# Causal attention in a six-layer kernel: the mask moves from TensorE products to GpSimd selects, and narrow score tiles share a PSUM bank

## The reference

```python
qkv = jnp.einsum('bsd,hde->bhse', x, Wqkv) + bqkv[None, :, None, :]
q, k, v = jnp.split(qkv, 3, axis=-1)
score = jnp.einsum('bhsd,bhtd->bhst', q, k)
causal = jnp.tril(jnp.ones((s, s), dtype=bool))
score = jnp.where(causal[None, None], score, -jnp.inf)
attn = jax.nn.softmax(score / jnp.sqrt(jnp.asarray(HEAD_DIM, x.dtype)), axis=-1)
y = jnp.einsum('bhst,bhtd->bhsd', attn, v)
y = jnp.transpose(y, (0, 2, 1, 3)).reshape(b, s, d)
out = y @ Wout + bout
```

## Time and profile before

| | |
|---|---|
| time, median of 3 runs | 1552.42 us (1550.23 to 1552.64) |
| time of the profiled execution | 1552.19 us |
| its span | 1550.4 us |
| busy over the span: PE, DVE, ACT, POOL | 94%, 64%, 49%, 29% |
| the layer's interleaved part | about 690 to 972 us of the span |
| exponentials L2232 | 384, 164.7 us busy |
| maxima L2277 | 304, 181.4 us busy |

### The profile page before, as it was taken

The page is one execution under the profiler, slowest core; times in us unless marked ns, Lnnn a source line. Parts: engine busy times, 40 slices in busy tenths (PEclk is TensorE's granted clock), DMA queues, the critical chain, the costliest instruction groups (busy, mean ns, idle before and its releaser), DMA issues. The chain is left out here.

```text
span 1550.4 us, 19613 instructions
## 1 busy us (share of the span) xinstructions
PE 1458.8 (94%) x7170; PEld 859.1 (55%) x7170; DVE 988.1 (64%) x1506; ACT 762.3 (49%) x1317; POOL 454.1 (29%) x348
## 2 busy tenths in 40 slices
PE   6999999989999899879999999899889999999998
PEld 3757765423232365444545443323568888888886
DVE  5774244778877634448887773677577574664753
ACT  5566345533434642725666665434655544445442
POOL 0046430142221410370000000201236656655562
PEclk9999999999999999989999999999999999999999
DMA  7000000000000000191553300000413222223201
GB/s 292 1 0 0 1 4 1 0 1 1 1 1 0 1 0 1 48 142 16 132 68 50 43 2 1 4 1 0 137 41 106 72 82 100 78 70 107 73 10 55
DMA packets 39047, 67.59 MB, mean 44 GB/s; under 512 B 3944, under 2 KB 19368, under 8 KB 38568
## 3 DMA queue, kind: packets, MB, share of 16 engines
q1 hardware_dynamic: 38952, 66.33, 16.1%
HBM read 57.80 MB, written 8.39 MB: 43 GB/s over the span
## 5 line engine op out<-in xcount | busy, mean ns | idle before, releaser
L2232 ACT ACTIVATE arena<-psum 128x512 f32<-128x512 f32 (+3 forms) x384 | 164.7, 498 | 118.8 <-PE psum L2082 85.1
L2277 DVE TENSOR_REDUCE b_mx<-psum 128x1 f32<-128x512 f32 (+3 forms) x304 | 181.4, 653 | 57.0 <-PE psum L2058 47.4
L3021 POOL TENSOR_TENSOR m_w_rest<-m_w,m_w_high 128x512 fp32r<-128x512 f32 (+1 forms) x88 | 111.6, 1270 | 154.7 <-ACT m_w_high L3220 154.7
L3471 DVE TENSOR_TENSOR m_hidden<-m_gelu,psum 128x512 f32<-128x512 f32 (+1 forms) x88 | 60.4, 686 | 147.7 <-ACT m_gelu L3312 124.5
L3114 PE MATMUL psum<-m_x_high,m_w_high 128*128 128x512 f32 (+1 forms) x352 | 137.9, 392 | 3.2 <-issue 3.2
L3027 POOL TENSOR_TENSOR m_h_rest<-m_hidden,m_h_high 128x512 fp32r<-128x512 f32 (+1 forms) x88 | 122.1, 1388 | 59.0 <-ACT m_h_high L3234 59.0
L3114 PE MATMUL psum<-m_x_rest,m_w_high 128*128 128x512 f32 (+1 forms) x352 | 137.7, 391 | 0.0
L3114 PE MATMUL psum<-m_x_high,m_w_rest 128*128 128x512 f32 (+1 forms) x352 | 137.6, 391 | 0.0
L3312 ACT ACTIVATE m_gelu<-psum 128x512 f32<-128x512 f32 (+1 forms) x88 | 52.4, 596 | 119.7 <-PE psum L3114 119.7
L1359 ACT ACTIVATE x_probs<-psum 128x1024 f32<-128x1024 f32 x56 | 57.3, 1023 | 90.4 <-PE psum L1097 90.4
L1517 DVE TENSOR_REDUCE x_mx<-psum 128x2 f32<-128x1024 f32 x64 | 76.6, 1218 | 35.0 <-PE psum L1071 34.8
(11 more groups left out here) (594 smaller groups left out, 3252.7 us busy)
## 6 DMA issues: line engine op xcount, KB each, us to landing
m_w<-w SPq DMA_DIRECT2D x32, 512.0 KB, 4.5
m_wo<-wo SPq DMA_DIRECT2D x16, 512.0 KB, 4.0
weights_sb<-weights SPq DMA_DIRECT2D x2, 2820.0 KB, 12.3
m_w<-w SPq DMA_DIRECT2D x16, 344.0 KB, 4.6
b_q_stack<-b_q_dram SPq DMA_DIRECT2D x36, 128.0 KB, 6.0
b_k_stack<-b_k_dram SPq DMA_DIRECT2D x36, 128.0 KB, 5.9
weights_sb<-weights SPq DMA_DIRECT2D x1, 3328.0 KB, 14.3
b_q_dram<-b_q_parts SPq DMA_DIRECT2D x6, 512.0 KB, 3.4
```

Of the source, the lines that this page charges most:

```text
L2232: act.activation(probs[slot % RING][:, 0:n], score(slot)[:, 0:n], ACT.Exp, scale=SCALE).then_inc(s["expd"].sem)
L2277: dve.tensor_reduce(mx[:, part, qi, heads[0]:heads[0] + nh], tile(("piece", p))[:, 0:nh * keys].rearrange("p (h n) -> p h n", n=keys), AX, ...
L3021: pool.tensor_tensor(w_rest[:, n % W_RING, :, :, 0:H_N(n % HT)], raw_of(n), w_high[:, n % W_RING, :, :, 0:H_N(n % HT)].bitcast(F32), ALU.s ...
L3471: dve.tensor_tensor(hidden[rows, n % 2, :], gelu[rows, n % 2, :], c.bank(2 + n % 2)[rows, :], ALU.mult)\
```

## The change

The product with `past` (L2082), and `past` itself, are gone. In its place GpSimd sets the exponentials of the future to zero: for each of the 64 diagonal groups one `affine_select` over the first 128 columns of its four tiles (128 x 4 x 128, f32, in place), after the group's last exponential and, by a new semaphore `masked`, ahead of its `values`.

Slots of 256 columns now share a bank two by two, and those of 128 four by four: `score_tiles` lists groups with the heads of one tile. One exponential takes the whole tile. A tile is issued at the slot of its first head; the slots of its other heads keep only what else stood there. So 304 exponentials take the place of 384. The three squares of GpSimd now stand among its selects.

```diff
--- before.py
+++ after.py
@@ -1782,6 +1782,11 @@
 
     groups = [(hs, ki) for hs in range(HALVES) for ki in range(4 * (hs % 2) + 4)]
     width = lambda ki, half: (half + 1) * CH - max(ki * P, half * CH)
+    diagonal_upto = lambda g: sum(ki >= 4 * (hs % 2) for hs, ki in groups[:g + 1])
+    together = lambda g: CH // width(groups[g][1], groups[g][0] % 2)
+    score_tiles = [(g, range(x, x + together(g))) for g in range(len(groups)) for x in range(0, QUAD, together(g))]
+    tiles_upto = lambda g: sum(of <= g for of, _ in score_tiles)
+    tile_at = {(g, heads[0]): i for i, (g, heads) in enumerate(score_tiles)}
     pairs_upto = lambda hs: 6 * (hs // 2) + (2 if hs % 2 == 0 else 6)
     first_group = lambda hs: 2 * pairs_upto(hs - 1) if hs else 0
 
@@ -1873,6 +1877,8 @@
         qs = [q_stack[:, 0], q_stack[:, 1], spare[:, 0]]
         ks = [k_stack[:, 0], k_stack[:, 1], spare[:, 1]]
         probs = [c.arena[:, i * CH:(i + 1) * CH] for i in range(RING)]
+        quad_of = lambda g: c.arena[:, QUAD * g % RING * CH:(QUAD * g % RING + QUAD) * CH].rearrange("p (h n) -> p h n", h=QUAD)
+        assert RING % QUAD == 0
         o, ot = c.slot(4), c.slot(5)
         o_t = o.rearrange("p a n -> p (a n)").rearrange("p (t n) -> p t n", t=TT)
         heads_out = c.ln[:].rearrange("p a n -> p (a n)")[:, 0:CH]
...
@@ -1962,13 +1968,10 @@
             def _(pool):
                 pool.memset(v_aug, 1.0).then_inc(s["ones"].sem)
                 c.clear_stale(pool)
-                pool.memset(future[:], 0.0)
-                pool.memset(past[:], 0.0).then_inc(s["masks"].sem)
+                pool.memset(future[:], 0.0).then_inc(s["masks"].sem)
                 pool.wait_ge(*s["masks"](1))
                 pool.affine_select(out=future[:], in_=future[:], compare_op=ALU.is_ge, fill=NEG, base=0,
-                                   pattern=[[-1, P]], channel_multiplier=1)
-                pool.affine_select(out=past[:], in_=past[:], compare_op=ALU.is_ge, fill=NEG, base=0,
-                                   pattern=[[1, P]], channel_multiplier=-1).then_inc(s["masks"].sem)
+                                   pattern=[[-1, P]], channel_multiplier=1).then_inc(s["masks"].sem)
                 pool.wait_ge(*s["masks"](2))
                 pool.memset(k_stack[ROWS:ROWS + SHIFT, :, :, :], 1.0).then_inc(s["k_ones"].sem)
                 for done in stored:
@@ -1987,11 +1990,28 @@
                 pool.wait_ge(*pr["v_proj"](8))
                 pool.memset(ks[2][ROWS:ROWS + SHIFT], 1.0).then_inc(s["k_ones"].sem)
                 pool.wait_ge(*s["k_ones"](2))
-                for ch in range(3):
+
+                def mask_future(g):
+
+                    pool.wait_ge(*s["expd"](tiles_upto(g)))
+                    to = quad_of(g)[:, :, 0:P]
+                    pool.affine_select(out=to, in_=to, compare_op=ALU.is_ge, fill=0.0, base=0,
+                                       pattern=[[0, QUAD], [1, P]], channel_multiplier=-1).then_inc(s["masked"].sem)
+
+                def next_square(ch):
                     pool.wait_ge(*s["read"](nth["mean", ch] + 1))
                     if ch == 2:
                         pool.wait_ge(*s["made"](nth["var", 0] + 1))
                     pool.tensor_tensor(next_squares(ch), chunk(xn_all, ch), chunk(xn_all, ch), ALU.mult).then_inc(yn["sq"].sem)
+
+                for g, (hs, ki) in enumerate(groups):
+                    if hs == HALVES - 2 and ki == 3:
+                        next_square(0)
+                    if ki >= 4 * (hs % 2):
+                        mask_future(g)
+                    if hs == HALVES - 2 and ki == 3:
+                        next_square(1)
+                next_square(2)
 
             @block.tensor
             def _(pe):
@@ -2065,27 +2085,28 @@
                         mm = pe.transpose(rows[:, t * P:(t + 1) * P], shift[:, hs % 2, t, :], ident16)
                     mm.then_inc(s["made"].sem)
 
-                def scores(slot):
-                    (hs, ki), h = groups[slot // QUAD], slot % QUAD
+                def scores(i):
+                    g, heads = score_tiles[i]
+                    hs, ki = groups[g]
                     a, half = hs // 2 % 3, hs % 2
-                    if ki == 0 and h == 0:
+                    if ki == 0 and heads[0] == 0:
                         pe.wait_ge(*shifted[hs % 2](SHIFT * 16 * (hs // 2 + 1)))
                         if hs == 4:
                             pe.wait_ge(*s["k_ones"](2))
-                    if slot >= SCORES:
-                        pe.wait_ge(*s["expd"](slot - SCORES + 1))
+                    if i >= SCORES:
+                        pe.wait_ge(*s["expd"](i - SCORES + 1))
                     q0, n = max(ki * P, half * CH), width(ki, half)
-                    diagonal = ki >= 4 * half
-                    mm = pe.matmul(score(slot)[:, 0:n], ks[a][0:ROWS + SHIFT, h, ki * P:(ki + 1) * P],
-                                   qs[a][0:ROWS + SHIFT, h, q0:q0 + n], start=True, stop=not diagonal)
-                    if diagonal:
-                        mm = pe.matmul(score(slot)[:, 0:P], ident16, past[:], start=False, stop=True)
+                    for x, h in enumerate(heads):
+                        mm = pe.matmul(score(i)[:, x * n:(x + 1) * n], ks[a][0:ROWS + SHIFT, h, ki * P:(ki + 1) * P],
+                                       qs[a][0:ROWS + SHIFT, h, q0:q0 + n], start=True, stop=True)
                     mm.then_inc(s["scored"].sem)
 
                 def values(pair):
                     hs, first_ki = groups[2 * pair]
                     b, quad, half = part_of(hs)
-                    pe.wait_ge(*s["expd"](QUAD * (2 * pair + 2)))
+                    pe.wait_ge(*s["expd"](tiles_upto(2 * pair + 1)))
+                    if first_ki >= 4 * half:
+                        pe.wait_ge(*s["masked"](diagonal_upto(2 * pair + 1)))
                     if first_ki == 0 and hs >= 1:
                         pe.wait_ge(*s["out_copied"](hs))
                     for i in range(2):
@@ -2148,7 +2169,8 @@
                 pe.wait_ge(*pr["v_copied"](8))
                 for slot in range(QUAD * len(groups)):
                     (hs, ki), x = groups[slot // QUAD], slot % QUAD
-                    scores(slot)
+                    if (slot // QUAD, x) in tile_at:
+                        scores(tile_at[slot // QUAD, x])
                     more_pieces(upto[slot], upto[slot + 1])
                     if x == QUAD - 1 and ki % 2 == 1 and slot // QUAD >= 3:
                         values(slot // QUAD // 2 - 1)
...
@@ -2223,13 +2245,16 @@
                 for t2 in range(4):
                     copy_value(1, t2)
 
-                def exps(slot):
-                    (hs, ki), h = groups[slot // QUAD], slot % QUAD
+                def exps(i):
+                    g, heads = score_tiles[i]
+                    hs, ki = groups[g]
                     n = width(ki, hs % 2)
-                    act.wait_ge(*s["scored"](slot + 1))
-                    if slot >= RING:
-                        act.wait_ge(*s["av"]((slot - RING) // QUAD // 2 + 1))
-                    act.activation(probs[slot % RING][:, 0:n], score(slot)[:, 0:n], ACT.Exp, scale=SCALE).then_inc(s["expd"].sem)
+                    act.wait_ge(*s["scored"](i + 1))
+                    if g >= RING // QUAD:
+                        act.wait_ge(*s["av"]((g - RING // QUAD) // 2 + 1))
+                    act.activation(quad_of(g)[:, heads[0]:heads[-1] + 1, 0:n],
+                                   score(i)[:, 0:len(heads) * n].rearrange("p (h n) -> p h n", n=n), ACT.Exp, scale=SCALE)\
+                       .then_inc(s["expd"].sem)
 
                 def copy_out(hs):
                     act.wait_ge(*s["av"](pairs_upto(hs)))
@@ -2239,7 +2264,8 @@
 
                 for slot in range(QUAD * len(groups)):
                     (hs, ki), x = groups[slot // QUAD], slot % QUAD
-                    exps(slot)
+                    if (slot // QUAD, x) in tile_at:
+                        exps(tile_at[slot // QUAD, x])
                     if hs >= 1 and ki == 2 and x == 1:
                         copy_out(hs - 1)
                 copy_out(HALVES - 1)
```

More of the change, by code:

```diff
@@ L1847, in causal_attention_layer @@
                                        loaded0=0, loaded1=0, loaded2=0, shifted0=0, shifted1=0, made=0, read=0,
-                                       max_step=0, parts=0, scored=0, expd=0, av=0, out_copied=0, inv=0))
+                                       max_step=0, parts=0, scored=0, expd=0, masked=0, av=0, out_copied=0, inv=0))
         set_round(0, s, pr)
@@ L1855, in causal_attention_layer @@
         future = sb("b_future", [P, P], BF16)
-        past = sb("b_past", [P, P], BF16)
         q_parts = sb("b_q_parts", [P, 3, FT, S], BF16)
@@ L1890, in causal_attention_layer @@
         norm_bank = lambda ch: c.bank(4 + ch)
-        score = lambda slot: c.bank(slot % SCORES)
+        score = lambda i: c.bank(i % SCORES)
         out_tile = c.bank(SCORES)
@@ L1915, in loads @@
```

(4 more changed lines are left out.)

## The result

The changed kernel takes 1534.15 us (1533.49 to 1545.4, 4 runs) against 1551.33 (4 runs), a ratio of 0.9903 with a 95% interval of 0.9881 to 0.9925. Forecast were 1536 us and 16.3 us less; 17.2 us less were measured. In a later comparison it was 1536.72 against 1553.86, 0.9892 (0.9877 to 0.9907).

What follows compares the result with a forecast made beforehand. PE's stream was taken to bound six of eight steps. Six steady steps gave 13.7 us, step 0 1.15 and step 7 1.46, together 16.3 us less: 1536 us, range 1532 to 1544.

Steps and rivals of the forecast that it cites:

- PE sets the pace: Steady steps: PE, busy 31.13 of 31.44 us, sets their time; each step saves 2.28 us.
- Wide products at 58 ns: Groups 512 and 384 wide: 16 products with past gone from PE, 0.93 us a step, less 0.1 for ACT.
- End of the even half: Narrow groups there: PE turns 0.43 us sooner and two masked scores go, 0.23 more; 0.66 us saved a step.
- End of the odd half: Narrow groups there: 2.41 us shrink to 1.62, ACT taking no part; 0.79 us saved a step.
- GpSimd's selects at nothing: Diagonal groups: a select takes 0.69 us, 0.7 to 1.4 with bounds, covered everywhere including the layer's end; cost 0.
- DVE at nothing: Steps: DVE's work stays 25.17 us and costs nothing, with 0.5 us a step as the bound.
- The rival by which a select shuts DVE out: Splitting of the shift held up by selects, up to 16.6 us, so no change, 1552; chance 0.06.
- Step 0: First step: nothing gained in the even half, where DVE sets the pace; 1.15 us in the odd one.
- End of the layer: Step 7's odd half: 0.35 us from products ahead of the projections, 0.45 from three heads behind the norm's product.
- The slower rival: Values of wide pairs wait for dearer selects: 16 us per microsecond beyond about 2.8, 1560 at 4.3; chance 0.07.

Runs made afterwards that it cites:

- e5: Changed kernel with the 256 products that mask the pieces left out too, maxima taken over the whole diagonal block: 1526.62 us, 0.9849.
- e1: Changed kernel without the shared tiles: every head has its own tile and exponential, GpSimd's selects stay in place of the products: 1544.25 us, 0.9959.
- e2: Changed kernel with the shared tiles alone: the products with past stay, no selects: 1544.51 us, 0.9957.
- e3: Changed kernel without the selects and the wait for them, exponentials of the future left in, so the mask is wrong: 1535.12 us, 0.9896.
- x3: Changed kernel with each of the 64 selects done three times, one after the other: 1543.0 us, 0.9949.
- x5: Changed kernel with each select done five times: 1604.39 us, 1.0339.
- e6: Changed kernel with the turning of the half before and its division moved from slot 1 to slot 3 of group 3: 1535.04 us, 0.9899.
- e7: Changed kernel with both maxima over the whole diagonal block and the turning moved to slot 3 of group 3: 1526.41 us, 0.9838.
- x3b: Changed kernel with each select done three times, but once in the last half: 1538.92 us, 0.9906.

## Why the prediction was right

The direction, the mechanism and the size held. Step by step:

- *PE sets the pace.* Shown. The steady steps lost 2.15 us each (forecast 2.28), with PE as full as before; e5 shows that this ends some 1 us further down.
- *Wide products at 58 ns.* Forecast 0.93 less 0.1 for ACT; measured 0.47 + 0.32 = 0.79. The odd half falls short of 0.46 by 0.14, where ACT and PE were forecast as level. ACT runs its eight exponentials there without a gap, 3.73 us from 793.40, which fits; no run makes ACT faster to show it.
- *End of the even half.* Forecast 0.66, measured 0.54. The term that was off is the turning: 1.66 us from the first score in place of 1.55. ACT's copy starts where it was forecast, 0.93 us behind the first score (0.92 before), and ends at 779.05; but PE turns only at 779.19, 0.14 later, where the sum had 0.03 for the way from ACT to PE.
- *End of the odd half.* Forecast 0.79, measured 0.81. e1 and e2 show that it needs both parts: 0.22 and 0.33 alone.
- *GpSimd's selects at nothing.* Shown by e3, and the cover by x3 for the steady steps. Forecast 0.69 us each, measured 0.64. At the end of the layer the cover is too thin for three selects, as x3 shows; a single one fits in it.
- *DVE at nothing.* It held in the steps. The rival by which a select shuts DVE out is real as a mechanism, below, but in the changed kernel the selects hardly meet the splitting: the one instruction that they hold up is the first of an odd half (L2314), 216 ns in place of 176, and PE's wait for the shift at the passage to the eighth step is 1.74 us with the selects and 1.70 without (e3). The prediction has it that no row before the change shows the mechanism; one does, that of L2291 in the last section.
- *Step 0.* From the first piece to ACT's first copy 45.9 us before and after (674.7 to 720.6; 683.6 to 729.5), though the clock was 0.89 there before and 0.85 after: this half gained nothing, as forecast. That DVE's own work sets its pace is only part of it. DVE stands still for 3.66 us of it before (3.90 after) beside GpSimd, and e5, with the same maxima, took 41.7.
- *Missed: 1.5 us at the passage to the eighth step.* From ACT's copy in the seventh step's odd half to that in the eighth's the sum had 1.81 (0.36 + 0.79 of the one half, 0.66 of the other), and it gave 3.31. Some 1.6 of that is the clock, for which the sum had no term. The steps' 0.13 each too much, 0.7 to 0.8 in six, hid half of it. So it is luck that the total, 17.0 us in the layer against 16.3, is nearer to the forecast than its terms; with the clock alike in both kernels it would have been about 15.4, still in the range.
- *End of the layer.* Forecast 0.35 + 0.45 = 0.80, measured 0.72 (from ACT's copy in the last half to the next layer, 31.16 us before and 30.44 after).
- *The slower rival's price.* It had 16 us for each microsecond over the cover. x5 shows it too low for a wait of this length: 2.6 us of waiting cost 4.3, as the clock falls behind the wait.

## What to carry to other kernels

Where PE's starts follow one another without holes, a small product costs the distance to the next start (58 ns for 128 columns here, though its record lasts 220), and moving it to an engine that stands still is worth that, if the new engine's result is wanted only much later; count the cover from the last input to the first use, and count it at the end of a stage apart, where nothing stands in between. Two edits that take away different limits of one place, here the product and the wait for a bank, give more together than alone. A wait put on TensorE is to be priced with what its clock may do behind it, and a gain of a microsecond or two is to be looked up in the clock of both profiles before the change gets it. Idle time on an engine isn't free room for another when the two can shut each other out: look what long instructions stand beside a short one that others wait for.

## What was not expected of the hardware

A wait of PE of 1.2 to 2.6 us can be followed by some microseconds at half the clock: 7 us at 0.50 in x3, 0.64 over 3.5 us in x5, 0.56 over 3.5 us in the kernel before. It doesn't have to be, and the length of the wait doesn't tell. At one and the same place, PE's wait for the shift at the passage to the eighth step, the profiles have:

| | PE waits, us | clock behind the wait |
|---|---|---|
| before, both profiles | 1.51, 1.50 | falls to 0.50 |
| e1, e2 | 1.50, 1.50 | 1.00 |
| changed, both profiles | 1.74, 1.74 | 1.00 |
| e3 | 1.70 | 1.00 |
| e6 | 1.73 | falls to 0.50 |
| e5 | 1.90 | 1.00 |
| e7 | 1.90 | falls to 0.50 |
| x3b | 2.16 | 1.00 |
| x3 | 2.16 | falls to 0.50 |

The fall lasts 3 to 4 us each time. What decides is open.

A short DVE instruction does stand still beside one of GpSimd. The same line (the splitting, `b_shift` from `b_mx` and `b_shift`, two SBUF inputs) in the changed kernel and in x3, where selects run beside it more of the time:

```profile
L2319 DVE SCALAR_TENSOR_TENSOR b_shift<-b_mx,b_shift x16: 174/175/176, 695.8 to 928.0; 128x16 bf16<-128x16 f32 x16
```

```profile
L2324 DVE SCALAR_TENSOR_TENSOR b_shift<-b_mx,b_shift x16: 174/486/551, 695.2 to 927.5; 128x16 bf16<-128x16 f32 x16
```

Its median goes from 175 to 486 ns, and the longest is 551, within one select of 637. The Trainium skill, SBUF — State Buffer, section "Who interferes with whom", says that a VectorE instruction with two SBUF inputs contends with a GpSimd one that reads SBUF; these rows agree with it. In the steady steps it cost nothing: DVE's busy time rose from 24.94 to 26.03 us, and the step stayed at 29.30. Where PE waits for the splitting, at the passage to the eighth step, it cost 0.42 us (2.16 in place of 1.74).

The dearest case was in the kernel before all along, in step 0. From the timelines of DVE and of GpSimd before the change:

```profile
682.99 3.66 DVE L2291 TENSOR_SCALAR b_shift<-b_mx 128x16 bf16<-128x16 f32 x1
```

```profile
682.57 4.05 POOL L1981 TENSOR_TENSOR arena<-arena,b_k_parts 128x2048 f32<-128x2048 f32 x1
```

An instruction of 0.17 us took 3.66 and ended with GpSimd's, though it has one tensor input and not two. In the changed kernel it was 3.90 us, in its second profile 1.96, each time what was left of the instruction of GpSimd. In e5 the splitting was through at 685.1, when GpSimd's 4.08 us had just begun (684.96), and PE turned the shift 8.4 us behind its first piece, where it was 12.3 before and 12.2 in the changed kernel's second profile.
